# Cross attention of a perceiver block: scores with the keys on the partitions, in plain float32, and the softmax put off to the batch's end

## What is computed

```python
def _L0_xattn_ref(x, context, Wq, Wk, Wv, Wo, bo):      # 8 heads of 64
    q = (x @ Wq).reshape(B, N, NUM_HEADS, HEAD_DIM).transpose(0, 2, 1, 3)
    k = (context @ Wk).reshape(B, M, NUM_HEADS, HEAD_DIM).transpose(0, 2, 1, 3)
    v = (context @ Wv).reshape(B, M, NUM_HEADS, HEAD_DIM).transpose(0, 2, 1, 3)
    attn = jax.nn.softmax(jnp.einsum('bhnd,bhmd->bhnm', q, k) * scale, axis=-1)
    out = jnp.einsum('bhnm,bhmd->bhnd', attn, v)
    return out.transpose(0, 2, 1, 3).reshape(B, N, INNER) @ Wo + bo
x = x + _L0_xattn_ref(_layernorm(x), ctx, ...)          # B=8, N=128, M=2048, inner 512
x = x + _L0_attn_ref(_layernorm(x), ...)
x = x + _L0_ffn_ref(_layernorm(x), ...)
```

## Time and profile before

| | |
|---|---|
| median of 3 runs | 1711.84 us (1708.66 to 1711.86) |
| the profiled execution, its own time | 1703.06 us |
| its span, first to last instruction | 1701.1 us |
| cross attention, first instruction to the last of VectorE's L591 | 1140.5 us |
| batch 0, and each later batch (by TensorE) | 183.9 us, then 136.5 us |
| busy: TensorE, ScalarE, VectorE, GpSimd | 96%, 39%, 38%, 32% |

### The profile page before, as it was taken

The page is one execution under the profiler, slowest core; times in us unless marked ns, Lnnn a source line. Parts: engine busy times, 40 slices in busy tenths (PEclk is TensorE's granted clock), DMA queues, the critical chain, the costliest instruction groups (busy, mean ns, idle before and its releaser), DMA issues. The chain is left out here.

```text
span 1701.1 us, 23083 instructions
## 1 busy us (share of the span) xinstructions
PE 1634.1 (96%) x9230; PEld 1290.6 (76%) x9231; DVE 648.4 (38%) x1079; ACT 663.5 (39%) x1196; POOL 541.3 (32%) x326
## 2 busy tenths in 40 slices
PE   7999999999999999999999999998889998999998
PEld 6667887887887888788788888773457686877876
DVE  6316325424523523632532542444365461222222
ACT  3225334434433533533433443342444433354421
POOL 6221132044043023124113304003620046768661
PEclk9999999999999999999999999999999998999999
DMA  5230121121111021021012112014200076656521
GB/s 209 88 99 26 39 68 50 32 74 50 32 63 46 17 81 50 26 73 59 25 32 75 50 32 81 1 36 170 75 1 1 21 259 143 172 148 188 162 56 35
DMA packets 70393, 125.15 MB, mean 74 GB/s; under 512 B 12000, under 2 KB 28448, under 8 KB 70304
## 3 DMA queue, kind: packets, MB, share of 16 engines
q1 hardware_dynamic: 40192, 92.14, 16.6%
q10 hardware_dynamic: 25296, 23.34, 4.7%
q0 software_dynamic: 4816, 8.41, 2.6%
HBM read 100.74 MB, written 24.43 MB: 74 GB/s over the span
## 5 line engine op out<-in xcount | busy, mean ns | idle before, releaser
L220 POOL TENSOR_TENSOR ctx_h<-stage,one 128x1024 fp32r<-128x1024 f32 x62 | 117.4, 1894 | 759.1 <-PE ps_t L288 759.1
L288 PE MATMUL ps_s<-ctx_h,wk 128*128 128x512 f32 x1024 | 325.4, 393 | 9.3 <-DVE ctx_l L498 9.3
L288 PE MATMUL ps_t<-wv,ctx_h 128*128 128x512 f32 x1024 | 317.7, 392 | 0.0
L542 DVE TENSOR_TENSOR kT<-ps_s,kT 64x512 fp32r<-64x512 f32 x128 | 87.5, 683 | 426.2 <-ACT kT L455 425.4
L288 PEld LDWEIGHTS ps_s<-ctx_h,wk 128*128 128x128 f32 x1024 | 193.5, 189 | 49.7 <-issue 9.9
L288 PEld LDWEIGHTS ps_t<-wv,ctx_h 128*128 128x128 f32 x1024 | 192.3, 188 | 42.3 <-issue 2.9
L564 DVE TENSOR_REDUCE smax<-ps_s 128x1 f32<-128x1024 f32 x128 | 150.6, 1218 | 142.1 <-PE ps_s L306 140.9
L288 PE MATMUL ps_s<-ctx_l,wk 128*128 128x512 f32 x512 | 200.3, 391 | 0.0
L288 PE MATMUL ps_t<-wv,ctx_l 128*128 128x512 f32 x512 | 199.3, 389 | 0.0
L438 ACT ACTIVATE probs<-ps_s,nmax 128x1024 f32<-128x1024 f32 x128 | 142.0, 1123 | 91.6 <-DVE nmax L567 91.6
L454 ACT ACTIVATE kT<-ps_s 64x512 fp32r<-64x512 f32 x128 | 75.6, 591 | 261.8 <-PE ps_s L288 168.3
(11 more groups left out here) (236 smaller groups left out, 2228.1 us busy)
## 6 DMA issues: line engine op xcount, KB each, us to landing
stage<-in_ctx_dram SPq DMA_DIRECT2D x64, 512.0 KB, 3.8
raw_u<-in_up_dram SPq DMA_DIRECT2D x32, 512.0 KB, 4.0
stage<-in_down_dram SPq DMA_DIRECT2D x16, 512.0 KB, 4.0
raw_e<-in_down_dram SPq DMA_DIRECT2D x16, 512.0 KB, 4.1
rows_scratch<-wxo SPq DMA_DIRECT2D x25, 256.0 KB, 4.6
wxo<-rows_scratch ACTq DMA_DIRECT2D x23, 256.0 KB, 3.4
q_scratch<-kT ACTq DMA_DIRECT2D x4, 1024.0 KB, 5.5
qa<-q_scratch ACTq DMA_DIRECT2D x32, 128.0 KB, 3.0
```

The lines of the kernel that those rows point to most:

```text
L220: nc.gpsimd.tensor_tensor(hi, raw, one[:, 0:1].unsqueeze(2).broadcast_to([P, 2, QT]), ALU.mult).then_inc(hi_done, 1)
L288: mm = nc.tensor.matmul(out, w(c), m(c), start=(c + k == 0), stop=(c == DC - 1 and k == 2))
L542: nc.vector.tensor_tensor(kT[XD:P, 0, p, keys], ps_s[0:XD, p, :], kT[0:XD, 0, p, keys], ALU.subtract)
```

## The change

- Order of the scores. A key projection is copied by ScalarE as plain float32 to `kT[:, p, :]` (all 128 partitions, two heads, only one group deep). `scores(b, g, p)` takes 128 keys as the stationary side and 128 queries as the moving side, so keys stand on the partitions. Head e of a pair uses partitions 64e to 64e + 63, that is one half of the array's rows; the two heads take turns, 8 matmuls in plain float32, in two PSUM banks. Queries are held once, unsplit (`qT`).
- No transposes of probabilities: `values` reads `s` as it is.
- Scores are stored (ScalarE, `copy_score`) in `s`, a tile of 8 heads x 16 x 128, and the softmax waits until the batch's last scores. VectorE keeps a running maximum in `top` (`max_scores`); at the end it is halved twice (`max_pair`), turned by TensorE (`turn_max`), reduced, put on a diagonal (`diagonal`) and spread over all partitions by a matmul with ones (`spread_max`). VectorE subtracts it from a whole head (`shift`), ScalarE takes the exponential in place (`exps`). Sums over the keys are adds on GpSimd (`tree`) and a matmul with ones (`sums`); of the last batch's second half, matmuls alone (`sums_of_chunks`).
- This end of batch b - 1 runs beside the first group of batch b. Values of b - 1 stand after the first eight projections of b; `vt` is a ring of 19 tiles.
- Scores are mixed among the projections, one group of 8 matmuls after each projection of some stretches.
- The high part of the context is made by ScalarE (`round_ctx`) in place of GpSimd. Storing the output and loading the queries move to SP's queue (one load of queries per batch in place of eight). At the opening, values are projected before keys, and the key weights are split after the value weights.

The diff, cut to its core:

```diff
+        RING = MT + 3
...
-        kT = sb("kT", [P, 2, PAIRS, M], F32R)
-        vt = sb("vt", [P, MT, D], F32)
-        qa = sb("qa", [P, XH, T], F32R)
-        qb = sb("qb", [P, XH, T], F32R)
-        probs = sb("probs", [P, 2, M], F32)
-        pT = sb("pT", [P, 2, MT, P], F32)
+        kT = sb("kT", [P, PAIRS, QT], F32)
+        vt = sb("vt", [P, RING, D], F32)
+        qT = sb("qT", [P, PAIRS, T], F32)
+        s = sb("s", [P, XH, MT, T], F32)
...
+        wq = s[:, 0:DC, 4:8, :].rearrange("p c a n -> p c (a n)")
+        xnT = s[:, DC:2 * DC, 4:8, :].rearrange("p c a n -> p c (a n)")
...
-        spare = [ps_v[:, 2, :], ps_o[:, :, :].rearrange("p h t -> p (h t)")]
+        ps_e = ps_s[:, :, :].rearrange("p k (i t) -> p k i t", i=4)
...
+        def max_room(p):
+            return ps_s[:, p, 0:2 * T] if p else ps_m[:, 0:2 * T]
...
+            def store_out(b):
+                sp.wait_ge(on_done, b + 1)
+                sp.dma_start(o_dram[b], on[:, :, :]).then_inc(o_stored, 16)
...
+            for b in range(1, B):
+                for k in range(4):
+                    next_ctx(b, k)
+                sp.wait_ge(s_done, nth_s(b, 0, 0))
+                load_queries(b)
...
+            def rest(lo, raw, hi, done):
                 nc.gpsimd.tensor_tensor(lo, raw, hi, ALU.subtract).then_inc(done, 1)
...
+            def tree(b, h):
+                room = tree_room(b)
+                parts = [s[:, h, 4 * i:4 * i + 4, :].rearrange("p c t -> p (c t)") for i in range(4)]
+                pool.wait_ge(exp_done, 2 * (b * XH + h + 1))
+                if b + h:
+                    pool.wait_ge(sum_done, b * XH + h)
+                if h == 0 and b:
+                    pool.wait_ge(l_done, b)
+                link(nc.gpsimd.tensor_tensor(room, parts[0], parts[1], ALU.add))
+                link(nc.gpsimd.tensor_tensor(room, room, parts[2], ALU.add))
+                link(nc.gpsimd.tensor_tensor(room, room, parts[3], ALU.add))
+                link(nc.gpsimd.tensor_tensor(room[:, 0:2 * T], room[:, 0:2 * T], room[:, 2 * T:4 * T], ALU.add))
+                nc.gpsimd.tensor_tensor(sum_room(b, h), room[:, 0:T], room[:, T:2 * T], ALU.add).then_inc(sum_done, 1)
...
-                split_ctx(0, k)
-            for b in range(1, B):
-                for k in range(LB):
+            for b in range(B):
+                for k in range(4, LB):
                     split_ctx(b, k)
+                if b < LASTB:
+                    for k in range(4):
+                        split_ctx(b + 1, k)
+                for h in range(XH if b < LASTB else XH // 2):
+                    tree(b, h)
...
-                def scores(h):
...
-                        keys = kT[:, h % 2, h // 2, j * 512:(j + 1) * 512]
-                        nc.tensor.matmul(ps_s[:, j, :], qa[:, h, :], keys, start=True, stop=False)
-                        mm = nc.tensor.matmul(ps_s[:, j, :], qb[:, h, :], keys, start=False, stop=True)
...
-                def transposes(h):
...
-                            pe.wait_ge((pT_even, pT_odd)[h3 % 2], AHEAD + b * MT + (4 * (h3 // 2) + j3 + 1))
-                        for i in range(4):
-                            mm = nc.tensor.transpose(ps_t[:, n % 3, i, :],
-                                                     probs[:, e, (4 * j + i) * P:(4 * j + i + 1) * P], ident[:, :])
-                        mm.then_inc(t_done, 1)
...
-                def values(p, part):
...
+            def project_k(b, g, p):
+                n = NTH[b, "K", g, p]
...
+                    pe.wait_ge(wk_split, 2)
+                h, l = ctx_h[:, g % 2], ctx_l[:, g % 2]
+                cols = slice(p * P, (p + 1) * P)
+                three(ps_p[:, n % 2, :], lambda c: wk[:, 0, c, cols], lambda c: wk[:, 1, c, cols],
+                      lambda c: h[:, c, :], lambda c: l[:, c, :],
+                      arrive_ctx(b, g) if p == 0 else None).then_inc(proj_done, 1)
...
+            def scores(b, g, p):
+                n = nth_s(b, g, p)
+                pe.wait_ge(k_copied, nth_k(b, g, p) + 1)
+                pe.wait_ge(q_in, (b + 1) * 16)
+                if n >= 2:
+                    pe.wait_ge(max_done, 2 * (n - 1))
+                for i in range(4):
+                    for e in range(2):
+                        rows = slice(e * XD, (e + 1) * XD)
+                        mm = nc.tensor.matmul(ps_e[:, 2 * (n % 2) + e, i], kT[rows, p, i * P:(i + 1) * P], qT[rows, p, :],
+                                              start=True, stop=True)
+                mm.then_inc(s_done, 1)
+            def turn_max(b, p):
+                pe.wait_ge(pm_done, b * PAIRS + p + 1)
+                if p:
+                    pe.wait_ge(max_done, 2 * (nth_s(b, NQ - 1, PAIRS - 1) + 1))
+                for e in range(2):
+                    mm = nc.tensor.transpose(max_room(p)[:, e * T:(e + 1) * T], top[:, p, e, 0, :], ident[:, :])
+                mm.then_inc(t_done, 1)
+            def spread_max(b, p):
+                pe.wait_ge(diag_done, b * PAIRS + p + 1)
+                nc.tensor.matmul(max_room(p), ones_r[:, :], diag[:, p % 2].rearrange("p e t -> p (e t)"),
+                                 start=True, stop=True).then_inc(m_spread, 1)
+            def values(b, p):
...
+            def sums(b, heads):
+                pe.wait_ge(sum_done, b * XH + len(heads))
+                for h in heads:
+                    mm = nc.tensor.matmul(sum_place(h), ones, sum_room(b, h), start=True, stop=True)
+                mm.then_inc(l_done, 1)
+            def sums_of_chunks(p):
+                for t in range(MT):
+                    for h in (2 * p, 2 * p + 1):
+                        nc.tensor.matmul(sum_place(h), ones, s[:, h, t, :], start=(t == 0), stop=(t == MT - 1))
...
+            def keys_and_scores(b, g, also=None):
                 for p in range(PAIRS):
...
-                pe.wait_ge(spread_done, b + 1)
+                    project_k(b, g, p)
+                    scores(b, g - 1, p)
+                    if also:
+                        also(p)
...
+            def values_and_scores(b, g, also=None):
+                for t in range(4):
+                    scores(b, g, t)
+                    project_v(b, g, t)
+                    if also:
+                        also(t)
...
+            def last_group(b):
+                def largest(t):
+                    if t == 1:
+                        turn_max(b, 0)
+                    if t == 2:
+                        spread_max(b, 0)
                 for p in range(PAIRS):
...
+            keys_and_scores(0, 1, lambda p: queries(PAIRS + p))
+            keys_and_scores(0, 2)
+            values_and_scores(0, 2)
+            last_group(0)
+            for b in range(1, B):
+                for p in range(PAIRS):
+                    project_k(b, 0, p)
+                    if p == 0:
+                        for i in range(1, PAIRS):
+                            turn_max(b - 1, i)
+                    else:
+                        spread_max(b - 1, p)
+                for t in range(4):
+                    project_v(b, 0, t)
+                for p in range(PAIRS):
+                    values(b - 1, p)
+                keys_and_scores(b, 1)
+                values_and_scores(b, 1, lambda t: sums(b - 1, range(XH)) if t == 1 else None)
+                for p in range(PAIRS):
+                    project_k(b, 2, p)
+                values_and_scores(b, 2)
+                last_group(b)
+            for p in range(1, PAIRS):
+                turn_max(LASTB, p)
+            for p in range(1, PAIRS):
+                spread_max(LASTB, p)
+            for p in range(PAIRS):
+                values(LASTB, p)
+                if p >= PAIRS // 2:
+                    sums_of_chunks(p)
+            sums(LASTB, range(XH // 2))
         @block.scalar
...
+            def copy_key(b, g, p):
+                act.wait_ge(proj_done, projected(b, "K", g, p))
+                n = nth_s(b, g, p) - PAIRS
+                if n >= 0:
+                    act.wait_ge(s_done, n + 1)
...
+            def copy_v(b, g, t):
+                act.wait_ge(proj_done, projected(b, "V", g, t))
+                if b:
+                    act.wait_ge(pv_done, PAIRS * (b if g or t == 3 else b - 1))
+                nc.scalar.activation(vt[:, nth_v(b, g, t) % RING, :], ps_p[:, NTH[b, "V", g, t] % 2], ACT.Copy) \
+                    .then_inc(v_copied, 1)
...
+            def copy_score(b, g, p):
+                n = nth_s(b, g, p)
+                act.wait_ge(s_done, n + 1)
+                if b and g == 0:
+                    act.wait_ge(pv_done, (b - 1) * PAIRS + p + 1)
+                    act.wait_ge(sum_done, (b - 1) * XH + 2 * (p + 1))
...
+                        act.wait_ge(q_stored, 16 * 2)
+                    if g == 3:
+                        act.wait_ge(xT_done, B)
+                for e in range(2):
+                    nc.scalar.activation(s[:, 2 * p + e, 4 * g:4 * g + 4, :], ps_e[:, 2 * (n % 2) + e], ACT.Copy) \
```

(80 more changed lines are left out.)

554 lines of the change are left out of this document (266 added, 288 removed).

## The result

The changed kernel takes 1637.8 us (median; 1633.79 to 1639.46) where the kernel before takes 1711.85 on the same chip (1708.66 to 1715.26): ratio 0.9564 [0.9538, 0.9589], 74 us or 4.4% less. The forecast was 1635. The profiled execution took 1637.4 with a span of 1635.5.

What follows compares the result with a forecast made beforehand. TensorE's queue was taken as the bound. Opening to 154.4, seven batches of 123.8, tail 37.4 and 5.2 for reciprocal and product end cross attention at 1063.6 against 1140.5; gain 76.9 off 1711.84 gives 1635 us, range 1605 to 1708.

Steps and rivals of the forecast that it cites:

- Scores, 0.88 us a group: TensorE's score groups: two heads on row halves overlap fully, 16 records at 54.8 ns, 14.0 us a batch.
- Rivals 1 and 2: Score row halves: 1, no overlap, 1752 us, chance 0.17; 2, partial overlap, 1676 to 1708 us, chance 0.05.
- Switching, 0.35: TensorE entering and leaving score groups among projections: 0.35 us each, 15 times a batch, 5.3 us.
- Batch 123.8: TensorE's sum for one cross-attention batch after the change: 123.8 us, 12.7 less than 136.5.
- the lock: VectorE instructions with only SBUF operands wait for a running GpSimd one; boundary scalings take 1.3 to 2.4 us each.
- The terms removed: TensorE work dropped per batch: score matmuls 14.6 us, transposes 14.2, matmuls spreading reciprocals 0.9.
- switching and waiting: Rest of the old 136.5 us batch on TensorE, about 6 us, between value blocks, transposes and scores.
- slack: Batch boundary: softmax ends at about 30 us, TensorE wants heads 6 and 7 at 34.5; 4 to 5 us.
- Rival 3: Another engine late at the batch boundary: 5 us a batch gives 1670 us, 10 gives 1705; chance 0.14.
- Opening: Before and in batch 0: today's extra 47.4 us stays, so its last value projection ends at 154.4 us.
- Tail, 37.4: Last batch's uncovered softmax, values and sums on TensorE after its last value projection: 37.4 us.
- the reciprocal: VectorE, end of the last batch: 512 elements at 8.8 ns each, 4.5 us.

Runs made afterwards that it cites:

- e2: Changed kernel with both heads' score matmuls reading the same half of the rows: 1740.99 us, a single run.
- e1: Changed kernel with the first head's four matmuls ahead of the second's in each score group: 1696.12 us, ratio 0.9952 to the kernel before.
- e4: Changed kernel with score groups two by two between pairs of projections, eight stretches a batch in place of fifteen: 1600.31 us, ratio 0.9395 to the kernel before.
- e3: Kernel before the change, with every transpose of the probabilities done twice into the same place: 1789.06 us, ratio 1.0503 to the kernel before.
- e6: Changed kernel with two extra VectorE reductions (4.5 us, results unused) at each batch boundary: 1637.36 us, a single run.
- e7: Changed kernel with six extra VectorE reductions (13.2 us, results unused) at each batch boundary: 1717.85 us, a single run.
- e10: As e4, but value stretches begin with scores too, so four score groups stand in a row once a batch: 1643.07 us, a single run.
- e9: As e7, but ScalarE's three value copies stand ahead of the exponentials of heads 2 to 7: 1679.72 us, a single run.
- e8: e4 with later spreading of maxima and the last batch's sums, reciprocal and product rearranged in parts: 1604.93 us, ratio 0.9362 to the kernel before.

## Why the prediction was right

The forecast of 1635 met 1637.8, and the profile shows the mechanism in its places. The scores themselves take as long as before (14.3 us a batch against 14.6); what pays is the transposes with their waits, less the excursions. By the prediction's own steps:

- **Scores, 0.88 us a group.** 0.89, records in pairs, in 1.1 us as said. This was the step with the most at stake, taken from the column halves of L374 without a row of its own, and it holds: e2 gives 1.78 for the case without overlap. Rivals 1 and 2 fall. It was not the rows alone: with the heads not in turn (e1) 8.6 of the 11.2 us a batch are lost again. The alternation in L374, which I named among the likenesses, was needed. The Trainium skill (TensorEngine Tiling (Array Packing), Key Properties) says that tiles load and multiply independently; the trace agrees for halves of rows, where the two heads are written in turn.
- **Switching, 0.35.** Too small: e4 gives 0.43, so 15 x 0.08 = 1.2 us a batch. It sat inside its bounds (0.10 to 0.46). The Trainium skill (the same page and section) says that a change of mode drains TensorE; the 0.43, and the excursions in full shape that cost nothing (e4), agree with it, and its weight was smaller than that of the work removed.
- **Batch 123.8.** 125.3. Switching is 1.2 more, the scores are 0.3 more, and 0.7 is lost at one place that I charged nothing for, a wait of 0.44 and a slower start behind it. Against these, the maxima and sums take 2.3 us by their starts where I had 3.3. The wait is the lock of the earlier trace rows: the first diagonals of a boundary (L746, SBUF operands alone) take 3.06 us for two beside GpSimd's split, 1.05 to 1.07 beside its adds and 0.48 in the tail, where GpSimd stands still, and TensorE waits 0.44 for them; in time, GpSimd, VectorE, TensorE:

```profile
528.94 4.75 POOL L281 TENSOR_TENSOR ctx_l<-stage,ctx_h 128x1024 fp32r<-128x1024 f32 x2 [22.65 <-ACT ctx_h L616]
...
530.72 3.06 DVE L746 TENSOR_SCALAR diag<-ident,mcol 128x128 fp32r<-128x128 f32 x2
...
533.83 0.39 PE L412 MATMUL ps_s<-diag,ones_r 128*128 128x256 f32 x1 [0.44 <-DVE diag L746]
```

- **What the removal gives.** The terms removed were right in sum; e3 shows that the transposes took 14 us of work as priced and 2.4 to 3.2 of waits, which I had under "switching and waiting" of about 6.
- **Other engines and the boundary.** Groups of the changed kernel (busy, mean ns, idle before):

```profile
L596 ACT ACTIVATE s<-s 128x1024 f32<-128x1024 f32 x128 | 125.8, 1050 | 5.9 <-DVE s L754 5.9
...
L754 DVE TENSOR_TENSOR s<-s,ps_s 128x2048 f32<-128x2048 f32 x48 | 106.1, 2275 | 0.0
...
L746 DVE TENSOR_SCALAR diag<-ident,mcol 128x128 fp32r<-128x128 f32 x64 | 41.9, 695 | 1.1
```

The shift was priced at 2.3 and takes 2.28 though GpSimd's trees run all the while (its second operand is in PSUM, as L542's). The exponential takes 1.05, not 1.12. The last exponentials of a boundary:

```profile
548.65 7.68 ACT L596 ACTIVATE s<-s 128x1024 f32<-128x1024 f32 x8
```

They end at 556.3, and TensorE comes to the last pair of values at 550.77 + 3 x 3.5 = 561.2: slack 4.9, where 4 to 5 was said. e6 uses 1.9 of it. Rival 3 falls for this kernel, but its mechanism is real: e7 costs 82 us, and more than the slack alone makes of it.
- **Opening.** 151.2 against 154.4. TensorE idles 9.5 us in it (151.20 - 141.69) where it idled 13.6 in the old one; I had carried 47.4 over whole. That values come first is the likely reason; it was not tried by itself.
- **Tail, 37.4.** 32.4. The exponentials of heads 4 and 5 end 18.6 us after the last projection (1046.7), not 22.5. In part that is the lock, to which I gave 2 us and which is hardly there, since GpSimd starts its adds only at 1032.9. Their values are done 21.2 after the last projection (1049.3), where I had 26. And the reciprocal:

```profile
1060.46 3.36 DVE L761 RECIPROCAL on<-ps_m 128x512 f32<-128x512 f32 x1 [11.44 <-PE ps_m L437]
1063.85 0.69 DVE L764 TENSOR_TENSOR on<-ps_o,on 128x512 f32<-128x512 f32 x1
```

3.36 in place of 4.5: 8.8 ns an element, from the difference of 8 and 4 elements, was too much; it is 6.5.

The end of the cross attention was to be at 1063.6 and is at 1064.5. That is closer than the terms are: 7 x 1.47 = 10.3 too little for the batches, 3.2 too much for the opening, 5.0 for the tail and 1.2 for the reciprocal, which leaves 0.9. The sum owes some of its fit to errors of both signs, and that is luck. The gain on the whole kernel, 74.0 by the medians, agrees with the 76.0 of the cross attention; that I took the predicted gain off the median and not off the profiled execution was right, since the two stood for different times of the untouched stages.

## What to carry to other kernels

Two matmuls with 64 rows of depth cost the time of one if they stand on different halves of the rows and are written in turn; read that off the starts in the trace, not by the length of a record (272 ns for nearly all of them in the changed kernel and in e2). Each excursion from full-array projections into half-array matmuls and back costs 0.43 us, so put such groups together, but no more of them in a row than there are free PSUM banks. And work put off to "somewhere under the next stage" is free only as far as the in-order queue of the engine that does it lets other copies pass: put what TensorE waits for ahead of what waits for another engine.

## What the runs showed of the hardware that I had not expected

- In e1 TensorE starts three records of the second head beside the first head's third and fourth matmul: 13 slots where one record after another would give 16 (which record is whose is my reading of their lengths).
- A stall of TensorE of 8.6 us is followed by about 5 us at half clock (e7, 0.52), so it costs 11.3. Shorter ones are followed by it too: 2.7 us in e10 (0.58 over the next 3.4 us) and 3.0 us in e9 (0.50 from 578.7 to 582.1, after a start at full clock). A batch's mean of 0.99 hides such a stretch.
- A reciprocal of 512 elements on VectorE takes 3.36 us, nearly five times a product of the same size (0.69): worth moving off a path that nothing covers, or cutting in two, as e8 does. A subtraction of 2048 elements with one operand in PSUM takes 2.28 us beside GpSimd's adds as well as without them (2.27 to 2.28 over all of them).
